# Token rows of two experts turned together, and gathers issued ahead of the scatters, in a graph-attention and mixture-of-experts kernel

## What is computed

```
x = x + relu(softmax(where(adj > 0, leaky_relu(f1 + f2.T), -9e15)) @ h)   h = layernorm(x) @ W; f1 = h @ a1; f2 = h @ a2
y = layernorm(x)                                                          1354 rows of 512
probs = softmax(y @ Wr + br); gate, idx = max, argmax over 8 experts
pos = rank of the row among the rows of its expert; kept where pos < 169  (so 168 rows an expert, as pos starts at 1)
expert_in[e, pos] = gate * y[row]
h = relu(expert_in @ W1[e] + b1[e]); eo = h @ W2[e] + b2[e]
x = x + gate * eo[idx, pos]
```

## Time and profile before

| | |
|---|---|
| median of 3 runs | 265.61 us (265.56 to 267.66) |
| profiled execution | 263.48 us |
| its span | 261.7 us |
| PE busy | 250.5 us, 96% |
| PEld, DVE, ACT, POOL busy | 210.8, 180.9, 128.6, 90.1 us |
| mean granted TensorE clock | 0.998 of full speed |
| of the chain that ended last | PE 87% |
| expert stage, 183.5 to 250.5 us | PE busy 67.00 of 67.00 us, DVE 46.28, ACT 31.43, POOL 32.21 |

### The profile page before, as it was taken

The page is one execution under the profiler, slowest core; times in us unless marked ns, Lnnn a source line. Parts: engine busy times, 40 slices in busy tenths (PEclk is TensorE's granted clock), DMA queues, the critical chain, the costliest instruction groups (busy, mean ns, idle before and its releaser), DMA issues.

```text
span 261.7 us, 4579 instructions
## 1 busy us (share of the span) xinstructions
PE 250.5 (96%) x1649; PEld 210.8 (81%) x1649; DVE 180.9 (69%) x429; ACT 128.6 (49%) x263; POOL 90.1 (34%) x113
## 2 busy tenths in 40 slices
PE   6799989999999999999999999999999999999990
PEld 1489989988888778778778889899977968879780
DVE  3988768996978977785762573847296685856931
ACT  2737786853765475555553121342447155454330
POOL 4334891000341432112120224118253834841502
PEclk9999999999999999999999999999999999999999
DMA  6990000320488888421211213136978679888001
GB/s 189 375 318 32 1 5 0 106 81 27 159 210 284 273 262 248 168 79 40 80 42 41 82 39 96 52 117 176 353 237 294 247 258 290 283 293 285 12 7 44
DMA packets 19210, 40.47 MB, mean 155 GB/s; under 512 B 2810, under 2 KB 3130, under 8 KB 19188
## 3 DMA queue, kind: packets, MB, share of 16 engines
q1 hardware_dynamic: 16196, 34.17, 39.5%
q0 software_dynamic: 2176, 4.80, 6.1%
q10 hardware_dynamic: 816, 1.21, 1.5%
HBM read 32.93 MB, written 8.31 MB: 158 GB/s over the span
## 4 chain that ended last, share of the span: by engine, by line
PE 87%; POOL 3%; DVE 2%; DMA 2%; issue 2%; ACT 2%; POOLq 1%; ACTq 0%
PE bank L1426 30%; PE bank L1690 12%; PE bank L1728 7%; PE bank L1364 6%; PE bank L1412 5%; PE bank L1756 5%; PE bank L1441 3%; PE bank L1660 2%; PE bank L1346 2%; DMA w_raw<-in_L_gnn_W_dram 2%; PE bank L1676 2%; PE bank L1703 2%; PE bank L1453 2%; PE bank L1464 2%; PE bank L1560 1%
## 5 line engine op out<-in xcount | busy, mean ns | idle before, releaser
L1426 PE MATMUL bank<-h_hi,pt_lo 128*128 128x512 f32 (+1 forms) x110 | 45.9, 417 | 0.0
L1426 PE MATMUL bank<-h_lo,pt_hi 128*128 128x512 f32 (+1 forms) x110 | 43.6, 396 | 0.0
L1426 PE MATMUL bank<-h_hi,pt_hi 128*128 128x512 f32 (+1 forms) x110 | 43.4, 394 | 0.0
L411 POOL TENSOR_TENSOR x_all<-x_all,w_raw 128x512 f32<-128x512 f32 x10 | 18.1, 1810 | 65.2 <-ACT w_raw L589 65.2
L1690 PE MATMUL bank<-prob,w 128*128 128x168 f32 x224 | 33.2, 306 | 0.0
L1690 PEld LDWEIGHTS bank<-prob,w 128*128 128x128 f32 x224 | 32.6, 189 | 0.7 <-issue 0.2
L754 ACT ACTIVATE adj_s<-bank,b_cols 128x168 f32<-128x168 f32 x28 | 11.3, 402 | 33.6 <-PE bank L1690 33.6
L1426 PEld LDWEIGHTS bank<-h_hi,pt_hi 128*128 128x128 f32 (+1 forms) x110 | 20.7, 188 | 4.9
L1426 PEld LDWEIGHTS bank<-h_hi,pt_lo 128*128 128x128 f32 (+1 forms) x110 | 20.7, 188 | 3.8
L1426 PEld LDWEIGHTS bank<-h_lo,pt_hi 128*128 128x128 f32 (+1 forms) x110 | 20.8, 189 | 3.6
L611 ACT ACTIVATE wide<-adj_s,off_b 128x1354 f32<-128x1354 f32 (+1 forms) x11 | 15.8, 1432 | 14.1 <-DVE off_b L887 14.1
(11 more groups left out here) (203 smaller groups left out, 558.1 us busy)
## 6 DMA issues: line engine op xcount, KB each, us to landing
w<-in_L_ffn_W_dram SPq DMA_DIRECT2D x16, 1024.0 KB, 6.7
adj_s<-in_adj_dram SPq DMA_DIRECT2D x10, 677.0 KB, 5.3
x_rows<-x_all SPq DMA_DIRECT2D x10, 257.0 KB, 3.2
out_dram<-x_all SPq DMA_DIRECT2D x10, 256.0 KB
x_all<-in_x_dram SPq DMA_DIRECT2D x9, 256.0 KB, 5.6
prob<-in_L_ffn_b_dram SPq DMA_DIRECT2D x5, 256.0 KB, 7.2
w_raw<-in_L_gnn_W_dram ACTq DMA_DIRECT2D x4, 256.0 KB, 5.5
adj_s<-in_L_ffn_b_dram SPq DMA_DIRECT2D x2, 256.0 KB, 7.0
```

The costliest lines, as they stand in the source:

```text
L411: pool.tensor_tensor(x_all[0:R, t, 0:D], x_all[0:R, t, 0:D], relu_s[0:R, :], ALU.add).then_inc(s_x1, 1)
L1426: ins = pe.matmul(o_ps[par][0:R, :], p[0:K, par, k, 0:R], h[0:K, k, :], start=(k == 0 and n == 0), stop=(k == NT - 1 and n == 2))
```

## The change

The wide block of an expert is still gathered, prepared and turned with its expert. The narrow blocks of experts e and e+1, e odd, are now prepared and turned together: `xg_n` holds the 40 rows of e on partitions 0 to 39 and those of e+1 on 64 to 103, and one block of 104 rows (`PAIR`, the 24 rows between them hold nothing that is used) is transposed. Experts 1 and 2, 3 and 4, 5 and 6 are such pairs; 7 has no partner and turns a block of 104 all the same. ACT copies each half to its own `gx_t`.

The narrow gathers of a pair count on a semaphore of their own (`s_x1n`), so `s_x1g[e]` counts the wide one alone from expert 1 on. POOL issues the narrow gather of e+1 with those of e, and in its loop the gathers now stand ahead of `scatter_out`. SP's first load of the stage waits for the wide gather of expert 1 alone.

```diff
@@ synchronize: SP @@
-            sp.wait_ge(s_x1g[1], 32)
+            sp.wait_ge(s_x1g[1], 16)
@@ what DVE has prepared up to expert e @@
+        def prepared(e):
+            return e + min(E - 1, e + e % 2)
@@ POOL @@
-            gather_x1(1)
-            gather_x1(2)
-            pool.wait_ge(s_x1g[1], 32)
+            gather_x1(1, 0)
+            gather_x1(1, 1)
+            gather_x1(2, 1)
+            gather_x1(2, 0)
+            pool.wait_ge(s_x1g[1], 16)
+            pool.wait_ge(s_x1n[0], 32)
             pool.wait_ge(s_xg, 2)
-            gather_x1(0)
+            gather_x1(0, 0)
+            gather_x1(0, 1)
             pool.wait_ge(s_dest, 1)
             for e in range(3, E + 2):
+                if e < E:
+                    pool.wait_ge(s_gt, e - 1)
+                    gather_x1(e, 0)
+                    if e % 2:
+                        gather_x1(e, 1)
+                        if e + 1 < E:
+                            gather_x1(e + 1, 1)
                 if e >= 4:
                     scatter_out(e - 4)
-                if e < E:
-                    pool.wait_ge(s_gt, e - 1)
-                    gather_x1(e)
@@ ACT, gx_copy(e) @@
+                act.wait_ge(s_gt, e + 1)
+                act.wait_ge(s_hid, 2 * e)
+                ins = act.activation(gx_t[e % 2][:, :, 0:P], gxw_ps[:, :].rearrange("p (c n) -> p c n", c=KC), ACT.Copy)
+                if e % 2:
+                    for i in range(min(2, E - e)):
+                        v = gxn_ps[:, 0:KC * PAIR].rearrange("p (c n) -> p c n", c=KC)
+                        ins = act.activation(gx_t[1 - i][:, :, P:CAP], v[:, :, P // 2 * i:P // 2 * i + S[1]], ACT.Copy)
                 ins.then_inc(s_gxt, 1)
@@ DVE, prepare(e) @@
-                dve.tensor_tensor(scale_s[:, par, :], x1_g[e][:, :, D + 1], gate_s[:, :, e], ALU.mult
+                dve.wait_ge(s_gt, max(e - 1, 1))
+                dve.wait_ge(s_x1g[e], 16)
+                dve.tensor_tensor(scale_s[:, par, 0:1], x1_g[e][:, 0, D + 1:D + 2], gate_s[:, 0, e:e + 1], ALU.mult
                                   ).then_inc(s_scale, 1)
-                dve.wait_ge(s_scale, e + 1)
-                for j in range(2):
-                    dve.tensor_scalar(xg[0:S[j], par, j, :], x1_g[e][0:S[j], j, 0:D], x1_g[e][0:S[j], j, D:D + 1],
-                                      scale_s[0:S[j], par, j:j + 1], ALU.subtract, ALU.mult).then_inc(s_xg, 1)
+                dve.wait_ge(s_scale, 2 + prepared(e - 1))
+                dve.tensor_scalar(xg_w[par], x1_g[e][:, 0, 0:D], x1_g[e][:, 0, D:D + 1], scale_s[:, par, 0:1],
+                                  ALU.subtract, ALU.mult).then_inc(s_xgt, 1)
+                if par:
+                    dve.wait_ge(s_x1n[e // 2 % 2], 32 * (e // 4) + 16 * min(2, E - e))
+                    for i in range(min(2, E - e)):
+                        dve.tensor_tensor(scale_s[0:S[1], 1 - i, 1:2], x1_g[e + i][0:S[1], 1, D + 1:D + 2],
+                                          gate_s[0:S[1], 1, e + i:e + i + 1], ALU.mult).then_inc(s_scale, 1)
+                    dve.wait_ge(s_scale, 1 + prepared(e))
+                    for i in range(min(2, E - e)):
+                        o = P // 2 * i
+                        dve.tensor_scalar(xg_n[e // 2 % 2][o:o + S[1], :], x1_g[e + i][0:S[1], 1, 0:D],
+                                          x1_g[e + i][0:S[1], 1, D:D + 1], scale_s[0:S[1], 1 - i, 1:2],
+                                          ALU.subtract, ALU.mult).then_inc(s_xgt, 1)
@@ PE, in_turn(e) @@
-                pe.wait_ge(s_xg, e * 2 + 2)
+                pe.wait_ge(s_xgt, prepared(e))
                 pe.wait_ge(s_gxt, e)
-                for j in range(2):
+                for c in range(KC):
+                    ins = pe.transpose(gxw_ps[:, c * P:(c + 1) * P], xg_w[e % 2][:, c * P:(c + 1) * P], ident[:, :])
+                if e % 2:
                     for c in range(KC):
-                        o = (c % 2) * CAP
-                        ins = pe.transpose(gx_ps[c // 2][:, o + j * P:o + j * P + S[j]],
-                                           xg[0:S[j], e % 2, j, c * P:(c + 1) * P], ident[0:S[j], 0:S[j]])
+                        ins = pe.transpose(gxn_ps[:, c * PAIR:(c + 1) * PAIR],
+                                           xg_n[e // 2 % 2][0:PAIR, c * P:(c + 1) * P], ident[0:PAIR, 0:PAIR])
```

More of the change, by code:

```diff
@@ L151, in gat_moe @@
             "p (j n) -> p j n", j=2) for v, n in ((wide, 2), (vecs, 1), (x_all, E - 3)) for i in range(n)]
-        xg = w_raw[:, :, 0:D].rearrange("p (i j) n -> p i j n", i=2)
+        xg_w, xg_n = (w_raw[:, 0, 0:D], w_raw[:, 2, 0:D]), (w_raw[:, 1, 0:D], w_raw[:, 3, 0:D])
+        PAIR = P // 2 + CAP - P
         gx_t = [prob[:, i, 0:KC * CAP].rearrange("p (c n) -> p c n", c=KC) for i in range(2)]
@@ L179, in gat_moe @@
         hid0_ps = (banks[2][:, 0:CAP], banks[2][:, CAP:2 * CAP], banks[3][:, 0:CAP], banks[6][:, 0:CAP])
-        gx_ps, hid_ps, eo_ps, y_ps = ((banks[0], banks[1]), (banks[2], banks[3]),
-                                      (banks[4], banks[5]), (banks[6], banks[7]))
+        gxw_ps, gxn_ps = banks[0], banks[1]
+        hid_ps, eo_ps, y_ps = (banks[2], banks[3]), (banks[4], banks[5]), (banks[6], banks[7])
         ya_ps, yb_ps = (banks[6], banks[4]), (banks[7], banks[5])
@@ L232, in gat_moe @@
         s_x1g = [sem(f"s_x1g{e}") for e in range(E)]
+        s_x1n = [sem("s_x1n0"), sem("s_x1n1")]
+        s_xgt = sem("s_xgt")
         s_end = [sem("s_end0"), sem("s_end1")]
@@ L438, in _, with gather_x1 @@
                                ALU.mult, ALU.mult).then_inc(s_sh2, 1)
-            def gather_x1(e):
-                for j in range(2):
-                    pool.indirect_dma_start(x1_g[e][0:S[j], j, :], None, x1_d,
-                                            bass.IndirectOffsetOnAxis(ap=src[0:S[j], j, e:e + 1], axis=0)
-                                            ).then_inc(s_x1g[e], 16)
+            def gather_x1(e, j):
+                pool.indirect_dma_start(x1_g[e][0:S[j], j, :], None, x1_d,
+                                        bass.IndirectOffsetOnAxis(ap=src[0:S[j], j, e:e + 1], axis=0)
+                                        ).then_inc(s_x1n[(e - 1) // 2 % 2] if j and e else s_x1g[e], 16)
             def scatter_out(e):
@@ L698, in _, with gx_copy_first @@
             exp_below(2)
-            def gx_copy(e):
[L701 to L704, removed]
-                for j in range(2):
[L706 to L712, removed]
+            def gx_copy_first():
+                for j in range(2):
+                    act.wait_ge((s_gt0, s_gt)[j], 1)
+                    act.activation(gx_t[0][:, 2 * j:2 * j + 2, :],
+                                   gx0_ps[j][:, 0:2 * CAP].rearrange("p (c n) -> p c n", c=2), ACT.Copy
+                                   ).then_inc((s_gx0, s_gxt)[j], 1)
+            def gx_copy(e):
+                act.wait_ge(s_gt, e + 1)
[5 more added lines that the diff above has]
+                        ins = act.activation(gx_t[1 - i][:, :, P:CAP], v[:, :, P // 2 * i:P // 2 * i + S[1]], ACT.Copy)
                 ins.then_inc(s_gxt, 1)
@@ L756, in hid_relu @@
                     ins.then_inc(s_hidv, 1)
-            gx_copy(0)
+            gx_copy_first()
             act.wait_ge(s_bc, 1)
```

8 lines of the change are left out of this document (1 added, 7 removed).

## The result

The changed kernel takes 267.63 us (median of 6 runs, 266.95 to 269.13) against 265.51 us for the kernel before (6 runs beside it). The ratio is 1.0112, with a 95% interval of 1.0064 to 1.0161. Timed once more, in 12 runs against 23, it is 268.78 us against 265.53, and 1.0141 (1.0099 to 1.0183). So it is slower by a little over 1%. The range held the time, but what happened is the first rival and not the forecast.

A forecast was written before the change was run, and what follows sets the result against it. PE alone was taken to bound the loop. From 263.48 us profiled, 0.9 gained in the loop and 1.7 lost in the opening gave 264.3, or 266.4 us as median; the range ran to 270.0 us.

The forecast's parts named there:

- the first rival: Opening: expert 2's narrow gather slips behind the weight load, costing 4.6 to 6.6 us; 269.3 to 271.3 us, chance 0.25.
- The bound: Loop: PE alone bounds it from 183 us on, 10.40 us per expert, while DVE, ACT and transfers stay ahead.
- The turns: PE's loop: three turns save 0.43 us each, three wider ones cost 0.13 each; gain 0.9 us, ends 0.4 and 1.5.
- the bound of 0.49: Turns without narrow rows: 0.49 us saved if the 0.17 us of issue goes too, less 0.05 to the next load.
- The opening, the issue: Expert 2's narrow gather on POOL: issue drawn out beside `w2_low(1)` on DVE to 1.68 us, ending at 179.46.
- The opening, the landing: Expert 2's narrow gather lands at 181.33, `in_turn(1)` at 182.80, `first_layer(1)` 1.7 us later, at 185.3.
- the flood: Opening: packets of SP's first weight load, issued 0.8 us earlier, fill the engines at about 181.2.
- What is hidden: DVE's odd `prepare` longer by 0.53 and some 0.2 us, ACT's copies by 0.3, gathers ahead of scatters: PE unaffected.
- The sum: Profiled execution: 263.48 - 0.9 + 1.7 = 264.3 us; median of the runs: 265.6 + 0.8 = 266.4 us.
- the forecast's own bounds: Loop gain 1.5 to 0.4 us and opening cost 0.4 to 3.0 us: 264.5 to 268.2 us.
- the half of the rival that the range took in: The range ran on into the second half of the first rival, to 270.0 us.
- the prediction's own limit of 1%: About 1%, 2.7 us, can be told from no change: 262.95 to 268.3 us counts as the same.

The follow-up runs named there:

- the moved `w2_low(1)`: Kernel before, with `w2_low(1)` moved behind `prepare(1)` and `eo_bias_high` on DVE; one run, 263.51 us.
- the restored wait: Changed kernel, with SP's first weight load waiting also for the narrow gathers of experts 1 and 2; 264.59 us, 0.9952 of the kernel before.
- pairs from two and `w2_low(1)` moved: Changed kernel with pairs 2 and 3, 4 and 5, 6 and 7, and `w2_low(1)` behind `eo_bias_high` on DVE; 263.16 us, 0.9964 of the kernel before.
- the early load in the kernel before: Kernel before, with SP's first weight load waiting only for expert 1's wide gather; 263.83 us, 0.9966.
- the kernel without pairs: Changed kernel with every expert turning its narrow rows alone, as a block of 104, opening as before; 263.11 us, 0.9942 of the kernel before.
- the narrow gathers first: Changed kernel with opening gathers ordered narrow 1, narrow 2, wide 1, wide 2; 265.03 us, 0.9999 of the kernel before.
- dummy products: Changed kernel with 15 products of 512 columns on PE ahead of `in_turn(1)`; 268.43 us in 4 runs, 1.0149 of the kernel before.

## Why the prediction was right or wrong

**The bound.** Right: in the loop what PE does is what counts, and no wait on DVE, ACT or a gather appeared there in the changed kernel.

**The turns.** Right in kind, too small: 0.9 us forecast, 2.1 measured, beyond the upper end of 1.5. Two terms were mis-sized. A turn without narrow rows saves 0.57 us, not 0.43. The whole 0.17 us of issue goes, and the next load does not start 0.05 us behind the wide ones, as the bound of 0.49 had it, but 0.03 us before their end. A turn with 104 in place of 40 was to cost 0.13 us and gives 0.14 to 0.19 back, for the same 0.17 us. I had taken that gap to belong to any second block and interpolated between block sizes, where it belonged to the 40-row block alone.

**The opening, the issue.** Right: drawn out to 1.75 us (1.68 forecast), and by DVE, as the moved `w2_low(1)` shows.

**The opening, the landing.** Here the forecast failed: "The landing comes out at 181.33." It was 184.46. The path behind it, 3.55 us from issue to DVE, is right when no load is in the way (3.57 measured). The mistake is in the time of the flood. I put it at 181.2 from the delay that the same load had shown, 2.1 us after its issue. But there the packets of a gather had begun 0.8 us after the load's issue, and the load's first ones came behind most of them. In the change, as in the four other runs with the load this early, no gather began in between, and the weights were moving 1.0 us after the issue, here from 179.55. The gather's issue ended at 179.36; with the load out of the way its first packets came 0.54 us after the end of its issue (181.75, against 179.47 + 1.74), so they would have come at 179.9. By this estimate the gather did not win by 0.2 us but lost by 0.3. That the load keeps it out is shown by the restored wait. That the order of the first packets decides was not tested, and the rule is not strict: with pairs from two and `w2_low(1)` moved, the load's first packets ran at 180.1, and 39 gather packets ran beside it between 181.0 and 182.25.

The rival had this wait right: 4.6 to 6.6 us forecast for the opening, 4.6 measured. It had a chance of 0.25 and was the case. That 4.6 is met so closely is in part luck: the landing came 0.4 us later after the first gather than its lower end (9.47 us against 184.18 - 175.16 = 9.02), and another term was too large by as much. From the turn to the first layer the forecast had 2.5 us (185.3 - 182.8), with the copies ending last; it was 2.15 (188.06 - 185.91), and 2.16 with the wait restored, which is also why the opening there cost 1.3 us and not 1.7.

**The clock.** Missing: no term of the sum or the rival had it, and it cost 1.1 us by the traces.

**What is hidden.** Right for the loop order of gathers and scatters (0.2 us between both orders), the longer odd `prepare` and ACT's third copy. The narrow gather of expert 2 alone decided.

**The sum.** The rival's 269.3 us held 0.9 us for the loop; with the 2.1 measured and 1.1 of clock it is 265.6 + 4.6 + 1.1 - 2.1 = 269.2, against 267.6 and 268.8 measured. For the profiled execution it is 263.48 + 3.6 = 267.1, and it took 266.95. The forecast itself was 0.8 us over before, where the medians say 2.12 and 3.25 and the profiles 3.47. Its errors partly cancel: 2.9 us too little for the opening, 1.1 for the clock left out, 1.2 too little for the gain of the loop, which takes its 264.3 us for the profiled execution to 267.1. So it is in part luck that the first measurement lies within the forecast's own bounds (268.2), and the second one (268.8) lies in the range for the half of the rival that the range took in. By the prediction's own limit of 1% the outcome is the slower one, which it gave 0.25, and not the one as fast as before, which it gave 0.72.

## What to carry to other kernels

When work is merged over two items, ask at the first pair what the second item's data is in the way of: in the loop it is early, at the start it is the newest request of all, and pairing from the second item on kept all of the gain. When a load's wait is weakened, every transfer whose packets have not begun when the load's do may stand behind all of it, so write down what is issued but not yet moving at that moment and who wants it next. And a delay read from the trace holds only with the company it had there: the same load's first packets came 2 us after its issue where a gather had begun to move in between, and 1 us after it where none had.

## What the runs showed of the hardware

- A load of 1 MB under way on one queue kept 40 gathered rows out for 3 us: no packet of the gather before 182.6, though its issue had ended at 179.36 and the weights took only 42.7% of the engines from 180.0 to 180.5. With the early load in the kernel before it was the same: no gather packet from 179.5 to 182.5. It is not always so complete: with pairs from two and `w2_low(1)` moved, 39 gather packets ran beside a load between 181.0 and 182.25.
- The load's first packets came 1.0 us after its issue where no gather was moving then, 1.3 us (the kernel without pairs) and 2.0 us (the kernel before) where a gather's packets had begun 0.5 and 0.8 us after the load's issue, and again 1.0 to 1.1 us with gather packets already moving within 0.2 us of it (the restored wait, the narrow gathers first).
- After a pause of 4.45 us PE ran for about a microsecond at full clock and then near 3.5 us at 1.2 GHz (in the repeat of the change it was at 1.2 GHz as soon as it went on, for 3 us). After one of 2.65 us it stayed at 2.4 GHz, and so it did after 3.40 us of dummy products and 1.62 us of pause.
- The weight loads of four transposes of 104 rows took 0.43 us, those of four of 40 rows 0.32 us with 0.17 us of issue before them.
- The clock also fell in a stretch where PE was busy 9.99 of 10 us (0.85 on average from 150 to 160), about 2 us of the span, in some executions of kernels that do the same there.
